# A two-layer vision network on one core: relative terms packed per head parity, and GpSimd adding the value products of the dilated attention

## Chip, cores and metric

The kernel runs on one core of a Trainium2 chip. The metric is the device time of one execution in microseconds (us), as the median of several runs. Engines are named as in the profile: PE is TensorE (PEld its weight loads), DVE is VectorE, ACT is ScalarE, POOL is GpSimd and SP is SyncE.

## What is computed

Four images of 64x64 tokens with 128 channels go through two layers. Layer 0 is a block attention with halo (8 heads of 16 channels, blocks of 8x8 queries, 12x12 keys) and a gated feed-forward part over the 2,047 best tokens. Layer 1 is a dilated attention (3x3 taps at dilations 2 and 3) and a graph attention over 524,288 edges that routes tokens to four experts. The change touches the two attentions only.

```python
# layer 0: scores of one block, plus relative terms
scores = einsum('bnhwqd,bnhwkd->bnhwqk', attn_q, key)       # q, k of 16 channels, k = 12*12
pos = rel_h[..., :, None] + rel_w[..., None, :]              # both from q and a 16x23 table
attn = softmax(scores + pos, axis=-1)
out = einsum('bnhwqk,bnhwkv->bnhwqv', attn, value)
# layer 1: nine dilated taps per pixel
attn = softmax(einsum('bndhw,bndkhw->bnkhw', qh, kw) * scale, axis=2)
out = einsum('bnkhw,bndkhw->bndhw', attn, vw)
```

## The kernel before

The program has these stages, one after the other on every engine: a sort of all edges (VectorE), then for each of the four images the first attention (`l0conv_*`), its feed-forward part (`l0ffn_*`), the dilated attention (`l1conv_*`) and the graph tables (`gat_*`); then the loop over the sorted edges, in which GpSimd gathers rows from HBM, and the last mixing of experts. Engines meet at a barrier after each part of an image. Within a part the order on each engine is the order of the code, and semaphores (`wait_ge`, `then_inc`) tie the engines together.

**First attention.** The 64 blocks of an image are 64 tiles `w`, with `h,i=w//8,w%8`: `h` is the row of blocks (called a strip here; the code's letter), `i` the block in it. All eight attention heads of a block are worked at once, four PSUM banks wide. Per tile PE runs `S(w+1)` (scores: 8 products of queries and keys, and 48 products that expand the relative terms), `weighted(w-1)` and `turn(w)` (transposes). After that comes a piece that depends on `i`: `values` in even tiles, `relative(h+1,a)` in tiles 1 and 3, `project` in tile 5, `queries` in tile 7. VectorE runs, per tile, the normalization of tile w (reciprocal and product, `norm`), the maximum over keys of tile w+1 (`mx`, L224), in tiles 2 to 5 one rounding remainder (`rest`), the copy of the transposed weights (L259) and the merge of the tile before. ScalarE takes the exponentials (L303). The scores have one set of banks, so `S(w+1)` waits for the exponentials of tile w.

`relative(h,a)` makes the relative term of a whole strip: 8 fp32 products of 64 columns with the tables `EH` (a=0) or `EW` (a=1). ScalarE copies it (L293), and it is split into three bf16 parts `ZZ[..][a][0..2]`, which the 48 products of `S` read with the indicator `INDB[a][o]`, where `o` is the parity of the attention head. Before the first tile of an image stands a prologue: queries, ten key chunks and both relative terms of strip 0.

**Dilated attention.** An image has 8 units `m`. Per unit VectorE makes 9 products of queries and shifted keys (`product`, L581), the softmax, and 9 products of expanded weights (PSUM) and shifted values (`value`, L587), eight of which it adds to an accumulator `ACC` (L590). PE sums the products into logits (L668), expands the weights for each tap (L686, four banks in turn) and projects a finished pair of units (L696, L699, bank 4). The products of unit m+1 are threaded between the values of unit m; unit 7 has none.

GpSimd issues in the meantime indirect DMAs: 128 gathers of sorted blocks during image 0 (L858, paced by `s_kv` and `s_p2`), and in images 1 to 3 32 scatters each (L954). The last 32 scatters come behind image 3.

Of the kernel before, what the change touches and what calls it, by code (L numbers as in the profile page):

```python
# [15 lines left out]
def declare_dense(nc, ctx, SA, SB):  # L16
# [759 lines left out]
def declare_nodes(nc,ctx,n,SA,m):  # L776
# [54 lines left out]
def pos_dve(dve,n,PSB,m):  # L831
# [18 lines left out]
    dve.drain()  # L850
def pos_pool(pool,m,n,d):

    I=m.SI
# [1 line left out]
    for t in range(NT):
        if t<20: pool.wait_ge(n.s_kv,t+1)
        else: pool.wait_ge(n.s_p2,(t-20)*66//108+1)
        pool.indirect_dma_start(out=I[:,t*BLK:(t+1)*BLK],out_offset=None,in_=d["SK"],in_offset=IOA(ap=m.BLKI[:,t:t+1],axis=0)).then_inc(n.gb_ld,16)  # L858
# [86 lines left out]
def edges_pool(pool,n,d,tick,V):  # L945

    pool.wait_ge(n.np_rdy,1)
    for t in range(NT):
        b,i=t//TILES,t%TILES
        if b<IMGS-1:  # L950
            if i==0: pool.wait_ge(n.ad_ld,16*(b+1))
            pool.wait_ge(n.s_p2,72*(b+1)+9*(i//4)+2*(i%4)+1)
        elif i==0: pool.wait_ge(n.ad_ld2,16)
        pool.indirect_dma_start(out=d["AEXP"],out_offset=IOA(ap=n.SIX[:,t:t+1],axis=0),in_=n.ADN[:,t,:],in_offset=None,bounds_check=4096*128-1,oob_is_err=False).then_inc(n.ad_sc,16)  # L954
# [650 lines left out]
```

## Time and profile before

| | |
|---|---|
| median of 3 runs | 7053.45 us (7039.84 to 7058.35) |
| the profiled execution | 7049.08 us, of which the span from first to last instruction is 7047.3 us |
| sort | 0 to about 980 us |
| first attention, per image | 36.8 us of prologue and 239.3 us of tiles in image 0 |
| dilated attention, per image | 199.3 to 212.7 us from the first softmax to the last residual |
| edge loop | about 3756 to 6600 us |
| last stage | about 6600 to 7047 us |

The profile's times are of one execution. "Busy" is the time in which an engine worked on an instruction; a row in brackets such as `[0.46 <-PE PSB L366]` gives the idle time of the engine just before, and the instruction whose end released it.

### The profile page before, as it was taken

Reading aid. Unit: us, or ns where it says so; the run is one execution under the profiler, and the core shown is the slowest. Engines: PE = TensorE matmul, PEld = TensorE weight load, DVE = VectorE, ACT = ScalarE, POOL = GpSimd, SP = SyncE. Lnnn points to the kernel's source line nnn. Section 1 sums busy time; section 2 is a strip of 40 time slices with the busy share of each in tenths; the row PEclk is TensorE's granted clock in tenths of the full one; section 3 lists DMA queues with packets and bytes.
Section 4 is the critical chain, followed back from the end, with each engine's and each line's share of the span. In section 5 each row is a group of like instructions: output and inputs, shape, how many; then the busy total and the mean of one; then the engine's idle time right before and its main releaser. Section 6 shows DMA issues by size and latency. Waiting matters only on the chain.

```text
span 7047.3 us, 83154 instructions
## 1 busy us (share of the span) xinstructions
PE 2995.6 (43%) x31245; PEld 1791.3 (25%) x31245; DVE 3414.0 (48%) x7000; ACT 1543.3 (22%) x3959; POOL 2605.7 (37%) x2472
## 2 busy tenths in 40 slices
PE   0011149766987897788760222222222222222204
PEld 0011138424842673376220000000000000000103
DVE  9999988576857685777661111111111111111138
ACT  0000027403730463165200111111111111111100
POOL 0000000051011000100017777777777777777450
PEclk9975569866986798698755656565655555555556
DMA  2000040002000100010022222222122222222216
GB/s 82 0 0 0 0 168 4 4 18 56 4 12 1 40 3 1 13 17 3 1 33 22 34 33 33 33 33 33 28 31 33 33 29 31 33 33 33 65 46 218
DMA packets 259879, 227.73 MB, mean 32 GB/s; under 512 B 115180, under 2 KB 223128, under 8 KB 250456
## 3 DMA queue, kind: packets, MB, share of 16 engines
q0 software_dynamic: 78944, 29.28, 6.6%
q1 hardware_dynamic: 99960, 99.91, 4.6%
q10 hardware_dynamic: 80640, 93.86, 4.3%
q8 instruction: 237, 3.88, 0.2%
q14 instruction: 98, 0.80, 0.0%
HBM read 100.42 MB, written 121.39 MB: 31 GB/s over the span
## 4 chain that ended last, share of the span: by engine, by line
PE 27%; issue 20%; another core or an unknown queue 19%; DVE 19%; DVEq 7%; ACT 4%; DMA 3%; POOL 1%; ACTq 1%; SPq 0%
DVE SA_ L1325 3%; PE PSB L382 2%; PE PSB L1175 2%; DVE SA_ L1315 2%; PE PSB L686 2%; PE PSB L668 2%; PE PSB L352 2%; PE PSB L526 2%; DVEq L1406 2%; PE PSB L392 1%; PE PSB L518 1%; DVE SA_ L590 1%; DMA VPAD<-s_TNT 1%; PE PSB L366 1%
## 5 line engine op out<-in xcount | busy, mean ns | idle before, releaser
L962 POOL DMA_INDIRECT SA_<-s_T,GIX x2048 | 2166.4, 1058 | 675.7 <-issue 675.7
L1175 PE MATMUL PSB<-VPAD,EH 128*128 128x512 f32 x512 | 302.0, 754 | 1994.1 <-DMA VPAD<-s_TNT 1643.1
L907 DVE TENSOR_TENSOR XPAD<-SA_ 128x256 f32<-128x256 f32 x32 | 13.6, 425 | 1789.9 <-DMA SA_<-s_T,GIX 1789.9
L954 POOL DMA_INDIRECT s_AEXP<-fill,SIX x128 | 149.6, 1169 | 1557.3 <-DVE SA_ L587 1472.2
L858 POOL DMA_INDIRECT SA_<-s_SK,BLKI x128 | 131.5, 1028 | 1484.3 <-PE PSB L710 1389.0
L1175 PEld LDWEIGHTS PSB<-VPAD,EH 128*128 128x128 f32 x512 | 121.6, 246 | 2195.3 <-DMA VPAD<-s_TNT 1681.4
L1179 PE MATMUL PSB<-SA_,EW 128*128 128x512 f32 x512 | 345.6, 824 | 342.1 <-ACT SA_ L1160 181.0
L1429 PE MATMUL PSB<-ident,SA_ 128*128 128x128 f32 x448 | 83.1, 368 | 837.1 <-DVE SA_ L1396 575.1
L303 ACT ACTIVATE PRX<-PSB,MX 128x144 f32<-128x144 f32 x1024 | 375.2, 380 | 210.3 <-DVE MX L224 210.1
L1164 ACT ACTIVATE VPAD<-PSB,PRX 128x512 f32<-128x512 f32 x128 | 87.9, 687 | 1308.8 <-remote 969.0
L1160 ACT ACTIVATE SA_<-PSB,PRX 128x512 f32<-128x512 f32 x256 | 175.9, 687 | 770.6 <-issue 327.0
L916 DVE TENSOR_TENSOR SB_<-SA_,SB_ 128x1024 f32<-128x1024 f32 x32 | 39.2, 1225 | 562.5 <-ACT SB_ L933 313.8
L1429 PEld LDWEIGHTS PSB<-ident,SA_ 128*128 128x128 f32 x448 | 77.4, 198 | 842.5 <-DVE SA_ L1396 579.0
L382 PE MATMUL PSB<-ident,PRX 128*72 128x128 f32 x2048 | 277.4, 279 | 1.0 <-DVE PRX L230 0.5
L1325 DVE TENSOR_TENSOR SA_<-SA_ 128x2048 f32<-128x2048 f32 (+1 forms) x124 | 254.3, 2051 | 8.6 <-issue 0.4
L1179 PEld LDWEIGHTS PSB<-SA_,EW 128*128 128x128 f32 x512 | 121.1, 250 | 539.7 <-issue 322.5
L1326 DVE TENSOR_TENSOR SA_<-SA_ 128x2048 f32<-128x2048 f32 (+1 forms) x124 | 253.4, 2044 | 0.0
L587 DVE TENSOR_TENSOR SA_<-PSB,VPAD 128x512 f32<-128x512 f32 x288 | 194.5, 685 | 119.0 <-PE PSB L686 119.0
L1347 ACT ACTIVATE SA_<-PSB 128x256 f32<-128x256 f32 x112 | 42.9, 383 | 875.6 <-PE PSB L1429 873.6
L259 DVE COPY VPAD<-PSB 72x512 f32<-72x512 f32 x256 | 175.6, 686 | 106.6 <-PE PSB L382 105.2
L382 PEld LDWEIGHTS PSB<-ident,PRX 128*72 128x72 f32 x2048 | 208.2, 116 | 53.2 <-issue 30.3
L224 DVE TENSOR_REDUCE MX<-PSB 128x4 f32<-128x576 f32 x256 | 192.9, 754 | 36.4 <-PE PSB L366 35.7
(365 smaller groups left out, 7339.3 us busy)
## 6 DMA issues: line engine op xcount, KB each, us to landing
SA_<-s_T,GIX POOLq DMA_INDIRECT x2048
s_Y<-VPAD ACTq DMA_DIRECT2D x32, 1024.0 KB
s_R<-zero SPq DMA_DIRECT2D x96, 256.0 KB, 2.9
s_R<-XPAD ACTq DMA_DIRECT2D x32, 768.0 KB
SB_<-s_Y SPq DMA_DIRECT2D x16, 1024.0 KB, 5.5
SA_<-s_Y SPq DMA_DIRECT2D x16, 1024.0 KB, 6.2
s_AEXP<-zero SPq DMA_DIRECT2D x32, 256.0 KB, 3.0
SA_<-in_x SPq DMA_DIRECT2D x16, 512.0 KB
```

Source lines behind the costliest of these rows:

```text
L224: dve.tensor_reduce(n.MX[:,w%2,:],PSB[:,0:2048].rearrange("p (j x) -> p j x",j=4)[:,:,0:144],AX.X,ALU.max,negate=True).then_inc(n.s_mx,1)
L259: dve.tensor_copy(n.PTS[:,4:8,:],PSB[0:72,5*512:6*512].rearrange("p (a q) -> p a q",a=4)).then_inc(n.s_ptd,1)
L303: last=act.activation(n.PR_[:,w%2,j,:],PSB[:,j*512:j*512+144],ACT.Exp,bias=n.MX[:,w%2,j:j+1],accum_out=n.SM[:,w%2,j:j+1])
L382: last=pe.transpose(PSB[0:72,o:o+P],n.PR_[:,w%2,j,72*g:72*g+72],ident)
L587: dve.tensor_tensor(rows(to),rows(PSB[:,bank*512:(bank+1)*512]),tap(n.VD,m,TAPS[j]),ALU.mult).then_inc(n.s_p2,1)
L962: pool.indirect_dma_start(out=n.G[:,s,c,:],out_offset=None,in_=d["T"],in_offset=IOA(ap=n.GIX[s][:,c:c+1],axis=0)).then_inc(n.gath[s],16)
L1160: act.activation(n.HM2[:,m,:],PSB[:,(m%4)*512:(m%4+1)*512],ACT.Gelu,bias=n.B1M[:,m:m+1]).then_inc(n.moe_ge,1)
L1175: pe.matmul(PSB[:,(m%4)*512:(m%4+1)*512],n.WM1[:,m//2,(m%2)*P:(m%2+1)*P],n.TNC[:,s,:],start=True,stop=True).then_inc(n.moe_h,1)
L1179: for f in range(2): last=pe.matmul(PSB[:,(4+e)*512:(5+e)*512],n.WM2[:,2*e+f,:],n.HM2[:,2*e+f,:],start=(f==0),stop=(f==1))
L1325: dve.tensor_tensor(x,a,b,ALU.min)
L1326: return dve.tensor_tensor(y,a,b,ALU.max)
L1429: last=pe.transpose(PSB[:,q*P:(q+1)*P],src[:,q*P:(q+1)*P],ident)
```

## The change

In the first attention each relative term is now made per head parity and not per table. ScalarE writes, behind the plain copy of the queries, two more copies that are masked to the even and odd heads (`QM`). `relative(h,o)` multiplies the masked queries of parity `o` with both tables, 16 products into one accumulation, with the tables' columns moved so that both lie side by side in a head pair's 32 rows. Then one indicator serves all, and `S` needs 24 products per tile where it had 48. The copy L293 becomes plain, since PE writes in the order of windows.

In the dilated attention VectorE writes the value products into a ring of four buffers `PR2` and no longer adds. GpSimd adds them (`l1conv_pool`), and issues its indirect DMAs between the adds: one gather per add in image 0 (48 gathers now come in the feed-forward part before, 20 in the key stage, 60 between adds), one scatter per two adds in images 1 to 3. `value` waits for the add four products back, and `project` for all adds of its pair of units.

```diff
+    n.PR2=[pr[:,6,:],pr[:,7,:],n.REST[:,:],SA[:,19968:20480]]
...
-        act.activation(n.QW[:,h%2,:].rearrange(WINDOWS,w=8,y=8),top.rearrange(ROWMAJOR,y=8,w=8),ACT.Copy).then_inc(n.s_qc,1)
+        act.activation(n.QW[:,h%2,:].rearrange(WINDOWS,w=8,y=8),top.rearrange(ROWMAJOR,y=8,w=8),ACT.Copy)
+        if h: act.wait_ge(n.s_p,b*16+2*h)
+        for o in range(2): last=act.activation(n.QM[o].rearrange(WINDOWS,w=8,y=8),top.rearrange(ROWMAJOR,y=8,w=8),ACT.Copy,scale=n.PAR[:,o:o+1])
+        last.then_inc(n.s_qc,1)
...
-        q=n.QW[:,h%2,:].rearrange(("c (w y x) -> c y w x","c (w y x) -> c x w y")[a],w=8,y=8)
-        for y in range(8):
-            last=pe.matmul(top[:,64*y:64*(y+1)],(n.EH,n.EW)[a][:,y,:],q[:,y,:,:],start=True,stop=True)
+        for t,form in ((n.EH,"c (w y x) -> c y w x"),(n.EW,"c (w y x) -> c x w y")):
+            q,out=(v.rearrange(form,w=8,y=8) for v in (n.QM[a],top))
+            for i in range(8):
+                last=pe.matmul(out[:,i,:,:],t[:,i,:],q[:,i,:,:],start=(i==0 and t is n.EH),stop=(i==7 and t is n.EW),skip_group_check=True)
...
-            for a in range(2):
-                for r,o,out in tiles: last=pe.matmul(out,n.ZZ[h%2][a][k][r,64*i:64*i+64],n.INDB[r,a,o,:],start=False,stop=(k==2 and a==1),skip_group_check=True)
+            for r,o,out in tiles: last=pe.matmul(out,n.ZZ[h%2][o][k][r,64*i:64*i+64],n.INDB[r,:],start=False,stop=(k==2),skip_group_check=True)
...
-        acc=n.ACC[:,m//2%2,m%2,:]; to=n.PR2[:,j%2,:] if j else acc
+        to=n.PR2[(j-1)%4] if j else n.ACC[:,m//2%2,m%2,:]
+        if j and 8*m+j>4: dve.wait_ge(n.s_ad,b*64+(8*m+j-4))
...
-        if j:
-            dve.drain()
-            last=dve.tensor_tensor(acc,acc,to,ALU.add)
-            if j==8: last.then_inc(n.s_acc,1)
...
-        if h==0: pe.wait_ge(n.s_acc,b*8+(2*u+2)); pe.wait_ge(n.s_cqc,b*8+min(2*u+5,8))
+        if h==0: pe.wait_ge(n.s_ad,b*64+8*(2*u+2)); pe.wait_ge(n.s_cqc,b*8+min(2*u+5,8))
...
+def l1conv_pool(pool,m,n,d,b):
+
+    if b: pool.wait_ge(n.ad_ld,16*b)
+    for u in range(UNITS):
+        acc=n.ACC[:,u//2%2,u%2,:]
+        for j in range(1,9):
+            k=8*u+(j-1)
+            pool.wait_ge(n.s_p2,b*72+(9*u+j+1))
+            pool.tensor_tensor(acc,acc,n.PR2[(j-1)%4],ALU.add).then_inc(n.s_ad,1)
+            if b==0 and HELD+PROJ+k<NT: block_pool(pool,m,n,d,HELD+PROJ+k)
+            if b and j%2==0: start_pool(pool,n,d,(b-1)*TILES+k//2)
+            pool.drain()
```

PE's queue in tile 1 of strip 0 in the first attention, from the scores of tile 2 to the start of those of tile 3, before. `PRX` are the weights, `VS` the values, `ident` marks transposes.

```order
L363 MATMUL PSB<-SB_,QW 64x144 x4
L363 MATMUL PSB<-SA_,QW 64x144 x4
L366 MATMUL PSB<-INDB,SA_ 64x144 x48
L392 MATMUL PSB<-VPAD,VS 32x128 x8
L382 MATMUL PSB<-ident,PRX 72x128 x8
L352 MATMUL PSB<-QW,EH 128x64 x8
L363 MATMUL PSB<-SB_,QW 64x144 x4
```

The same place in the changed kernel, where `VPAD` in the rows of L356 is the region that holds the first masked copy.

```order
L367 MATMUL PSB<-SB_,QW 64x144 x4
L367 MATMUL PSB<-SA_,QW 64x144 x4
L369 MATMUL PSB<-INDB,SA_ 64x144 x24
L395 MATMUL PSB<-VPAD,VS 32x128 x8
L385 MATMUL PSB<-ident,PRX 72x128 x8
L356 MATMUL PSB<-VPAD,EH 128x8x8 x8
L356 MATMUL PSB<-VPAD,EW 128x64 x8
L367 MATMUL PSB<-SB_,QW 64x144 x4
```

The score piece has 24 products less, and the relative piece between the transposes and the next score piece has 16 products where it had 8.

VectorE's queue in the dilated attention, from the third value product of a unit to the next softmax, before.

```order
L587 TENSOR_TENSOR SA_<-PSB,VPAD 128x512
L590 TENSOR_TENSOR SA_<-SA_ 128x512
L587 TENSOR_TENSOR SA_<-PSB,VPAD 128x512
L590 TENSOR_TENSOR SA_<-SA_ 128x512
L581 TENSOR_TENSOR SA_<-QW,SB_ 128x512
L587 TENSOR_TENSOR SA_<-PSB,VPAD 128x512
L590 TENSOR_TENSOR SA_<-SA_ 128x512
L587 TENSOR_TENSOR SA_<-PSB,VPAD 128x512
L590 TENSOR_TENSOR SA_<-SA_ 128x512
```

The same place after, to the softmax itself (`REST` is one of the four ring buffers).

```order
L591 TENSOR_TENSOR SA_<-PSB,VPAD 128x512
L591 TENSOR_TENSOR REST<-PSB,VPAD 128x512
L584 TENSOR_TENSOR SA_<-QW,SB_ 128x512
L591 TENSOR_TENSOR SA_<-PSB,VPAD 128x512 x3
L591 TENSOR_TENSOR REST<-PSB,VPAD 128x512
L591 TENSOR_TENSOR SA_<-PSB,VPAD 128x512
L602 TENSOR_REDUCE LMX<-PSB 128x32
```

The adds have left VectorE's queue. They stand in GpSimd's, here at its start in image 0.

```order
L854 DMA SA_<-s_SK,BLKI 128x64 x68
L880 ISA
L880 TENSOR_TENSOR SA_<-SA_ 128x512
L854 DMA SA_<-s_SK,BLKI 128x64
L880 TENSOR_TENSOR SA_<-SA_ 128x512
L854 DMA SA_<-s_SK,BLKI 128x64
L880 TENSOR_TENSOR SA_<-SA_,REST 128x512
```

68 gathers now stand ahead of the first add, and each further gather stands behind an add.

## Rows read from the trace of the kernel before

**Rows 1.** Windows: us, busy PE, PEld, DVE, ACT, POOL, granted clock, DMA.
```profile
1018.80:1258.10 239.30, 225.70 (x6056) 189.99 (x6060) 193.70 (x427) 177.81 (x653) 0.00 (x0) 0.99 0.17 60
2114.90:2327.50 212.60, 154.84 (x498) 55.16 (x498) 155.62 (x275) 18.04 (x31) 34.86 (x32) 0.62 0.01 1
3756.00:6600.00 2844.00, 626.14 (x992) 235.98 (x992) 335.21 (x1121) 351.95 (x462) 2166.39 (x2049) 0.58 0.21 32
```

**Rows 2.** Groups: busy, mean ns, idle before and its releaser.
```profile
L224 DVE TENSOR_REDUCE MX<-PSB 128x4 f32<-128x576 f32 x256 | 192.9, 754 | 36.4 <-PE PSB L366 35.7
L590 DVE TENSOR_TENSOR SA_<-SA_ 128x512 f32<-128x512 f32 x256 | 177.2, 692 | 24.3 <-issue 0.9
```

**Rows 3.** Timeline, strip 3, tiles 4 and 5 of image 0: start, us, engine, instruction.
```profile
1124.78 0.17 DVE L228 RECIPROCAL RSM<-SM 128x4 f32<-128x4 f32 x1
1125.70 0.75 DVE L224 TENSOR_REDUCE MX<-PSB 128x4 f32<-128x576 f32 x1
1126.82 2.06 PE L352 MATMUL PSB<-QW,EW 128*128 128x64 f32 x16
1128.35 0.18 DVE L228 RECIPROCAL RSM<-SM 128x4 f32<-128x4 f32 x1
1128.81 0.35 PE L363 MATMUL PSB<-SB_,QW 32*64 32x144 f32 x4
1129.11 0.68 PE L366 MATMUL PSB<-INDB,SA_ 32*64 32x144 bf16 x48
1129.82 0.76 DVE L224 TENSOR_REDUCE MX<-PSB 128x4 f32<-128x576 f32 x1 [0.46 <-PE PSB L366]
```

**Rows 4.** L366: who waited for it (us, times).
```profile
  DVE MX L224: 35.7, 64
```

**Rows 5.** L382: what ended PE's idle time before it (us, times).
```profile
  issue: 30.3, 153
  DVE PRX L230: 22.5, 106
```

**Rows 6.** Timeline of image 1's prologue.
```profile
1708.80 0.60 ACT L281 ACTIVATE QW<-PSB 128x512 f32<-128x512 f32 x1 [3.86 <-DMA s_ADT<-VPAD]
1711.97 0.61 ACT L293 ACTIVATE REST<-PSB 128x512 f32<-128x512 f32 x1
1712.94 2.06 PE L352 MATMUL PSB<-QW,EW 128*128 128x64 f32 x16
1714.83 3.95 PE L346 MATMUL PSB<-XPAD,WK 128*128 128x476 f32 x10
1715.84 2.25 ACT L285 ACTIVATE SB_<-PSB,PAR 128x476 f32<-128x476 f32 x3 [0.94 <-PE PSB L346]
```

**Rows 7.** Timeline of units 2 and 3, image 1's dilated attention.
```profile
2184.74 0.69 DVE L587 TENSOR_TENSOR SA_<-PSB,VPAD 128x512 f32<-128x512 f32 x1 [0.36 <-PE PSB L686]
...
2189.25 0.45 DVE L602 TENSOR_REDUCE LMX<-PSB 128x32 f32<-128x288 f32 x1
...
2199.34 1.29 DVE L587 TENSOR_TENSOR SA_<-PSB,VPAD 128x512 f32<-128x512 f32 x2 [2.61 <-PE PSB L686]
...
2207.32 0.69 DVE L587 TENSOR_TENSOR SA_<-PSB,VPAD 128x512 f32<-128x512 f32 x1 [1.33 <-PE PSB L686]
...
2214.25 0.45 DVE L602 TENSOR_REDUCE LMX<-PSB 128x32 f32<-128x288 f32 x1
```

**Rows 8.** Timeline of unit 7, image 1.
```profile
2303.50 1.29 DVE L587 TENSOR_TENSOR SA_<-PSB,VPAD 128x512 f32<-128x512 f32 x2 [3.92 <-PE PSB L686]
...
2315.37 2.04 PE L696 MATMUL PSB<-BPR,ones 1*128 1x512 f32 x2 [4.30 <-issue]
```

**Rows 9.** GpSimd's gathers: VectorE idle (first row), and beside its products.
```profile
1399.22 0.94 POOL L858 DMA_INDIRECT SA_<-s_SK,BLKI  x1 [0.30 <-issue]
...
1433.76 1.29 DVE L581 TENSOR_TENSOR SA_<-QW,SB_ 128x512 f32<-128x512 f32 x2
1433.98 1.28 POOL L858 DMA_INDIRECT SA_<-s_SK,BLKI  x1 [0.30 <-issue]
```

More of the change, by code:

```diff
@@ L70, in declare_dense @@
     n.s_gt, n.s_tb, n.x3_st, n.tn_st, n.t_st, n.sorted_ = [sem(s) for s in ("s_gt", "s_tb", "x3_st", "tn_st", "t_st", "sorted_",)]
-    n.s_acc, n.s_ltc, n.s_lt, n.s_res = [sem(s) for s in ("s_acc", "s_ltc", "s_lt", "s_res",)]
+    n.s_ad, n.s_ltc, n.s_lt, n.s_res = [sem(s) for s in ("s_ad", "s_ltc", "s_lt", "s_res",)]
     n.s_ka, n.s_kd, n.s_p, n.s_pe, n.s_c0, n.s_r, n.s_c1, n.s_z = [sem(s) for s in ("s_ka", "s_kd", "s_p", "s_pe", "s_c0", "s_r", "s_c1", "s_z",)]
-    n.INDB=sb("INDB",[P,2,2,144],bf16)
+    n.INDB=sb("INDB",[P,144],bf16); n.G4=sb("G4",[P,128,4]); n.QM=[V[:,4352:4864],n.G4[:,:,:].rearrange("p t e -> p (t e)")]
     n.bar=dict(pe=n.bar_pe,act=n.bar_act,dve=n.bar_dve)
@@ L100, in sync_weights @@
     for h in range(8):
-        for t,nm in ((n.EH,"pos_emb_h"),(n.EW,"pos_emb_w")):
+        for t,nm,o in ((n.EH,"pos_emb_h",h//2*32),(n.EW,"pos_emb_w",h//2*32+16)):
             for q in range(8):
-                ld(t[16*h:16*h+16,q,16*h:16*h+12],d[nm][:,11-q:23-q])
+                ld(t[16*h:16*h+16,q,o:o+12],d[nm][:,11-q:23-q])
     n.NW=loads
@@ L112, in dve_prep @@
     dve.tensor_scalar(n.PAR4[:,:],n.PAR[:,:],0.25,None,ALU.mult)
-    for a,ind in enumerate((n.INDH,n.INDW)):
-        for o in range(2): dve.tensor_scalar(n.INDB[:,a,o,:],ind[:,:],n.PAR[:,o:o+1],None,ALU.mult)
+    dve.tensor_scalar(n.INDB[:,:],n.INDH[:,:],n.PAR[:,0:1],None,ALU.mult); dve.drain()
+    dve.scalar_tensor_tensor(out=n.INDB[:,:],in0=n.INDW[:,:],scalar=n.PAR[:,1:2],in1=n.INDB[:,:],op0=ALU.mult,op1=ALU.add)
     dve.tensor_copy(n.DIGI[:,:],iota[:,0:16]); dve.drain()
@@ L199, in kbank @@
     return PSB[:,KB[c%6]*512:KB[c%6]*512+hi-lo]
-ROWMAJOR="p (y w x) -> p w y x"; COLMAJOR="p (x w y) -> p w y x"; WINDOWS="p (w y x) -> p w y x"
+ROWMAJOR="p (y w x) -> p w y x"; WINDOWS="p (w y x) -> p w y x"
 def l0conv_first_dve(dve,n,b):
@@ L292, in relative @@
         if h or a: act.wait_ge(n.s_z,b*16+(2*h+a))
-        act.activation(n.REST[:,:].rearrange(WINDOWS,w=8,y=8),top.rearrange((ROWMAJOR,COLMAJOR)[a],w=8,y=8),ACT.Copy).then_inc(n.s_pe,1)
+        act.activation(n.REST[:,:],top,ACT.Copy).then_inc(n.s_pe,1)
         act.drain()
@@ L850, in pos_dve, with block_pool, keys_pool @@
     dve.drain()
+HELD=48; PROJ=20
+def block_pool(pool,m,n,d,t):
+    pool.indirect_dma_start(out=m.SI[:,t*BLK:(t+1)*BLK],out_offset=None,in_=d["SK"],in_offset=IOA(ap=m.BLKI[:,t:t+1],axis=0)).then_inc(n.gb_ld,16)
 def pos_pool(pool,m,n,d):
-    I=m.SI
     pool.wait_ge(m.blk_rdy,1); pool.wait_ge(m.sk_st,16)
[L855 to L858, printed above, removed]
+    for t in range(HELD+PROJ):
+        if t<HELD: pool.wait_ge(n.s_h,t*2//3+1)
+        else: pool.wait_ge(n.s_kv,t-HELD+1)
+        block_pool(pool,m,n,d,t)
+def keys_pool(pool,m,n,d):
     pool.wait_ge(n.end_rdy,1)
@@ L862, in pos_pool, with start_pool @@
         if t>=4: pool.wait_ge(n.s_h,32+t-3)
-        pool.indirect_dma_start(out=I[:,t*128:(t+1)*128],out_offset=None,in_=rows,in_offset=IOA(ap=m.QI[:,t:t+1],axis=0)).then_inc(n.a2_ld,16)
+        pool.indirect_dma_start(out=m.SI[:,t*128:(t+1)*128],out_offset=None,in_=rows,in_offset=IOA(ap=m.QI[:,t:t+1],axis=0)).then_inc(n.a2_ld,16)
+def start_pool(pool,n,d,t):
+    pool.indirect_dma_start(out=d["AEXP"],out_offset=IOA(ap=n.SIX[:,t:t+1],axis=0),in_=n.ADN[:,t,:],in_offset=None,bounds_check=4096*128-1,oob_is_err=False).then_inc(n.ad_sc,16)
+def l1conv_pool(pool,m,n,d,b):
[9 more added lines that the diff above has]
+            pool.drain()
 def edges_prep_dve(dve,n,SA,V,ones,K,row):
@@ L945, in edges_pool @@
 def edges_pool(pool,n,d,tick,V):
[L947 to L954, printed above, removed]
+    pool.wait_ge(n.ad_ld2,16)
+    for t in range((IMGS-1)*TILES,NT): start_pool(pool,n,d,t)
     pool.wait_ge(n.d0_rdy,1)
@@ L1505, in _ @@
             pos_pool(pool,m,n,d)
+            l1conv_pool(pool,m,n,d,0)
+            keys_pool(pool,m,n,d)
+            pool.wait_ge(m.fill_done,FILLS); pool.wait_ge(n.np_rdy,1)
+            for b in range(1,IMGS): l1conv_pool(pool,m,n,d,b)
             V=blocks(pool,m)
-            pool.wait_ge(m.fill_done,FILLS)
             edges_pool(pool,n,d,m.tick,V)
```

4 lines of the change are left out of this document (2 added, 2 removed).

## The prediction

> **What bounds the kernel now.** I read the windows first, to see which stages the change can reach [rows 1]. The edge loop takes 2,844 us, its gathers and their order stay as they are, and so do the sort and the last stage: nothing there. What moves is the first attention (239.3 us of tiles in image 0, after a prologue) and the dilated attention (212.6 us in image 1), in each of four images. In the first, PE is busy 225.7 of 239.3 us at a granted clock of 0.99; in the second, VectorE is busy 155.6 of 212.6 us, and PE 154.8 us at a mean clock of 0.62, that is, in part at 1.2 GHz. So the two halves of the change meet two different limits. In the first attention the change must take work off PE, or off the loop that runs through PE, VectorE and ScalarE. In the second it takes work off VectorE, and the reader has to ask where VectorE then waits for PE or GpSimd.
>
> **First attention: the scores.** The 48 indicator products take 0.68 us [rows 3], so 24 less are worth 0.34 us a tile, and 256 tiles would give 87 us if each were bound by them. The groups say how seldom that is so: the maximum L224 waits for them 35.7 us in all, in 64 of 256 tiles [rows 2, 4]. In the other tiles the maximum follows the normalization of the tile before, which takes 0.92 us from the reciprocal to the maximum (1124.78 to 1125.70 [rows 3]) and starts when the exponentials are done, just as the scores do; the scores need 1.0 us (1128.81 to 1129.82). With them at 0.67, the normalization is what ends last. The second gain would be that the transposes come 0.34 us earlier; but in 106 tiles they already waited for the normalization, and in the 153 others (an idle of 0.20 us each) they stand close behind it [rows 5]. So outside the tiles named next I take about 0.1 us a strip, nearly nothing.
>
> **First attention: the relative terms.** This is the term that speaks against the change. `relative` goes from 8 products to 16. The trace shows 16 records for 8 fp32 products, and the next tile's scores start 1.99 us after the first (1126.82 to 1128.81 [rows 3]), with PE not idle before them. Each record has its own load of a 128x128 table, and their number doubles, so I take another 1.95 us (the EH form is some 0.1 us shorter). In this place PE is what ends last: the reciprocal that follows the exponentials stood at 1128.35, before the scores, and the maximum then waited 0.46 us for PE [rows 3]. These are the 56 tiles (2 in each of strips 0 to 6, four images) that make up most of the 64 waits [rows 4]. What the doubled piece adds lies on the path: +1.95 for the relative piece, -0.34 for the shorter scores behind it, +1.6 us. Behind this stall, what is late next is the copy of the transposed weights, the merge and the normalization: a chain that keeps its length, so nothing is made up. 56 x 1.6 = +90 us.
>
> **Prologue.** Here both relative pieces stand in a chain with the key chunks, and ScalarE has two more copies at about 0.55 us spacing ahead of the first. The queries are now ready at 1709.4; with the masked copies at 1710.6. The first piece then takes to 1714.6, where ScalarE now copies at 1711.97; the second starts after that copy, at 1715.7 in place of 1712.94, and ends at 1719.8, so the keys start 4.9 us later than 1714.83, for which ScalarE already waits 0.94 us [rows 6]. The masked copies of strip 1's queries, ahead of the first exponentials, add 1.1 us. Sum +6 us an image, +24 us. In tile 0 of a strip the masked copies hold up an exponential by some 0.2 us at most and are in the 90.
>
> Sum for the first attention: 90 + 24 - 2 = **+112 us**. Lower end: every tile but the 56 gains its full 0.34 us (200 x 0.34 = 68 us), which leaves +47. Upper end: no gain from the shorter scores at all (56 x 1.95 = 109), the prologue, and 7 us of ScalarE: +140.
>
> **Dilated attention: what VectorE loses.** The 256 adds are 177.2 us [rows 2]. Most of this isn't on the path. In unit 3 of image 1 the first value product waits 2.61 us for PE, and the fifth at 2207.32 again 1.33 us; without adds it comes to that point earlier and waits longer, since PE runs without a gap at the low clock before it. What is left of the gain is the end: from 2207.32 to the next softmax at 2214.25 are 6.93 us for five values and their adds, and five values alone take 5 x 0.69 = 3.4, a gain of 3.5 us. In a unit that closes a pair (units 2, 4 and 6) the projection holds the last three values: 2184.74 to 2189.25 is 4.51 us, and 3 x 0.69 = 2.1 leaves a gain of 2.4 us [rows 7]. The seven units with a successor: 4 x 3.5 + 3 x 2.4 = 21 us an image, 85 us in all, if GpSimd costs nothing.
>
> **What GpSimd costs.** The trace has no GpSimd add. Lower bound: VectorE's 0.69 us [rows 2]. Upper bound: I take 1.5 us, a fifth over the spacing of GpSimd's gathers, 1.25 (0.94 and 0.30 of issue [rows 9]). I choose 1.2, by the nearest row of that engine. A unit then needs 8 x (1.2 + 1.25) = 19.6 us in image 0 and 8 x 1.2 + 4 x 1.3 = 14.8 us in the others. Unit 7 has no products to fill the time, and `project` waits for its last add: from the second value at about 2304.2 GpSimd needs 14.8 us, to 2319, and the projection started at 2315.37 [rows 8]. So the end of each image is 4 to 5 us later, +18 in all.
>
> Then contention. A gather on GpSimd takes 0.94 us with VectorE idle and 1.28 beside VectorE's products of two SBUF inputs [rows 9]. The Trainium skill (SBUF — State Buffer, Who interferes with whom) says that a VectorE instruction with two SBUF inputs and a GpSimd instruction that reads SBUF exclude each other for the whole instruction; the row shows a stretch, not a whole block, and has no add. Mechanism and price here: after the last value of a unit up to four adds are outstanding, while VectorE runs the softmax with two products and one multiply of two SBUF inputs on its path. If each waits for half an add, 3 x 0.6 = 1.8 us a unit; if none, 0. I take 1.3 us, 28 units, +36 us.
>
> Sum for the dilated attention: -85 + 18 + 36 = -31; the gathers that now stand between adds in image 0 bring its unit near 22 us of the 23 to 26 it has, where GpSimd itself begins to bind, and I take 6 us off the gain: **-25 us**. Ends: adds at 0.69 us and no contention, with unit 7 some 3 us shorter, -97; every product that meets an add waits for a whole one (3 x 1.2 a unit, 101 us in place of 36), +40.
>
> The Trainium skill (GPSIMD Engine Reference, Elementwise — side-by-side cycle accounting) gives 4,497 ns for an add of 2,048 fp32 columns; a quarter, 1.12 us, is an estimate from that page. By it a unit's adds would take 0.6 us less, and the sum would be about 2 us lower.
>
> **Sum.** 112 - 25 = +87 us on the profiled execution's own 7049 us: 7136. The median of the runs is 4 us above that execution, so 7140.
>
> **Rivals.**
>
> *Contention makes the dilated attention slower too* (chance 0.13). For it: the softmax path has three exposed instructions, and image 0 has a gather per add. Against: products 2 to 5 have 2.61 us of cover, 6 to 8 more. It gives +112 + 10 to 40: 7170 to 7200.
>
> *The first attention takes only half of my cost* (0.19). For it: PE's transposes came earlier in 153 tiles, and the loads of the tables might overlap better when 16 follow each other. Against: the 16 records now follow each other at 0.12 us with nothing between. It gives +50 to 70, less 25 to 50: 7053 to 7098.
>
> *Faster* (0.07). PE's clock is what decides. It stands at 0.62 in the dilated attention; a VectorE that leaves shorter gaps may keep PE at 2.4 GHz for most of a unit. Then the waits of 2.61 and 1.33 us shrink, and a unit goes toward VectorE's own work: 18 products x 0.69 and some 4.4 us of softmax and residual, 16.8 us in place of 25. It decides where the dilated attention gains more than the first loses, 112 / 28 = 4 us a unit net of the ends; at 6 us a unit it is 168 - 112 = 56 us faster, 6997. Against: PE's long idle during the softmax, after which it stands at half clock, stays.
>
> *The relative terms aren't dearer*, as the name of the change may suggest (24 products in place of 48) and PE gets lighter: refuted by the counts, 64 pieces x 1.95 = +125 us of PE against 87.
>
> **How the numbers follow.** The forecast's own case (first attention +90 to +140, dilated -60 to 0) has 0.61: 7083 to 7190. A measurement of this kernel tells 0.3%, 21 us, from no change. Faster than 7032: the third rival and a sliver of the second, 0.08. Within 21 us: the low part of the second rival, 0.13. Slower: 0.79. The range leaves out about 0.1 on either side: 7055 to 7192.
>
> **What the changed profile would show.** Relative pieces of 32 records and about 3.95 us, with the next scores right behind; waits of the maximum for PE of about 2 us in 56 tiles, over 100 us in all where it has 35.7; 63 tile periods of an image in about 261 us in place of 239.3; a prologue 6 us longer. In the dilated attention: units of 22 to 24 us, GpSimd adds near 1.2 us, VectorE products longer or started late where an add runs, and 4 to 5 us more before the last projection. Wrong would be I if a relative piece took 2.5 us, if an add took over 2 us (then GpSimd binds every unit), or if PE's clock rose above 0.8 there.

## The result, and the profile after

The changed kernel takes 7209.32 us (median of 4 runs, 7205.4 to 7213.07), the kernel before, run beside it, 7048.49 (7039.84 to 7058.35): a ratio of 1.0228, 95% interval 1.021 to 1.0245. It is slower by 161 us. The profiled execution spans 7203.6 us against 7047.3: +156.

The stages of both traces, read off the timelines (first product of queries, first and last maximum L224 of an image, first softmax maximum L602 of unit 0 and of unit 7, last residual), images 0 to 3 in order. The prologue counts here from the first product of queries; "36.8 us" for image 0 in the table of the kernel before also holds what stands ahead of that product.

| stage | before, us | after, us | change |
|---|---|---|---|
| first attention, prologue | 17.2, 18.4, 17.2, 17.2 | 20.6, 24.7, 28.1, 21.0 | +24 |
| first attention, tiles 0 to 63 | 239.3, 237.1, 238.5, 237.0 | 257.3, 257.7, 257.9, 257.1 | +78 |
| feed-forward part | 76.1 each | 87.9, then 76.1 to 76.3 | +12 |
| dilated attention, units 0 to 6 | 176.9, 180.2, 166.8, 178.3 | 223.8, 158.2, 158.4, 161.1 | +47 in image 0, -48 in the others |
| dilated attention, unit 7 and ends | 35.8, 32.4, 32.4, 32.4 | 51.8, 42.4, 42.2, 41.8 | +45 |

The rest (key stages, edge loop, last stage) is the same within 3 us in all. After, the windows of the first attention of image 0 and of the dilated attention of images 1 and 0 answer to [rows 1]:

```profile
1023.40:1280.60 257.20, 239.44 (x4764) 202.72 (x4768) 191.39 (x427) 185.51 (x667) 0.00 (x0) 0.99 0.14 49
2243.70:2444.30 200.60, 137.23 (x498) 50.96 (x498) 124.67 (x211) 17.99 (x31) 120.28 (x96) 0.67 0.01 1
1458.20:1733.80 275.60, 148.98 (x498) 56.17 (x498) 121.82 (x211) 18.07 (x31) 143.27 (x124) 0.61 0.03 7
```

VectorE's busy time in the dilated attention fell from 155.6 to 124.7 us, and GpSimd's rose from 34.9 to 120.3. Image 1 gained 12 us by it; image 0, with the same VectorE time, lost 63.

In the first attention the stall came in the tiles that were forecast. Strip 3, tile 5, in the timeline of image 0, beside [rows 3]:

```profile
1132.44 1.90 PE L356 MATMUL PSB<-VPAD,EH 128*128 128x64 f32 x16
1134.17 2.09 PE L356 MATMUL PSB<-VPAD,EW 128*128 128x64 f32 x16
1136.19 0.35 PE L367 MATMUL PSB<-SB_,QW 32*64 32x144 f32 x4
1136.49 0.48 PE L369 MATMUL PSB<-INDB,SA_ 32*64 32x144 bf16 x24
1137.00 0.76 DVE L224 TENSOR_REDUCE MX<-PSB 128x4 f32<-128x576 f32 x1 [2.20 <-PE PSB L369]
```

32 records and 3.75 us from the first to the next scores, where there were 16 and 1.99; the maximum waits 2.20 us for PE instead of 0.46. Over the kernel, the groups beside [rows 2] (busy, mean ns, idle before and its releaser):

```profile
L224 DVE TENSOR_REDUCE MX<-PSB 128x4 f32<-128x576 f32 x256 | 192.7, 753 | 124.5 <-PE PSB L369 124.5
L880 POOL TENSOR_TENSOR SA_<-SA_ 128x512 f32<-128x512 f32 x192 | 256.4, 1335 | 1269.2 <-DVE SA_ L591 1123.5 <-issue 127.0 <-DVE REST L591 18.7
L584 DVE TENSOR_TENSOR SA_<-QW,SB_ 128x512 f32<-128x512 f32 x288 | 229.4, 844 | 20.4 <-PE PSB L668 20.1
L591 DVE TENSOR_TENSOR SA_<-PSB,VPAD 128x512 f32<-128x512 f32 x224 | 149.1, 686 | 201.1 <-PE PSB L686 114.6 <-POOL SA_ L880 86.5
```

The wait of L224 for PE went from 35.7 us in 64 tiles to 124.5 in 66. The last row is new: VectorE's value products now wait 86.5 us for a buffer that a GpSimd add must free (and 47.1 us more for the buffer `REST`), and the products of QW and keys take 844 ns where they took 685.

How far the adds lie apart is seen in image 0's timeline (GpSimd and the value products):

```profile
1575.09 1.26 POOL L880 TENSOR_TENSOR SA_<-SA_ 128x512 f32<-128x512 f32 x1 [1.64 <-issue]
1576.45 0.69 DVE L591 TENSOR_TENSOR SA_<-PSB,VPAD 128x512 f32<-128x512 f32 x1 [3.30 <-POOL SA_ L880]
1576.49 0.95 POOL L854 DMA_INDIRECT SA_<-s_SK,BLKI  x1
1578.98 1.26 POOL L880 TENSOR_TENSOR SA_<-SA_,REST 128x512 f32<-128x512 f32 x1 [1.54 <-issue]
```

An add takes 1.26 us and a gather 0.95, as expected. But the next add starts 1.5 to 1.6 us after the gather has ended: 3.9 us from add to add where the prediction had 2.45. Over the whole kernel the pause between an indirect DMA and the next add, where GpSimd waited for nothing else, has a median of 1.47 us and is mostly between 1.3 and 1.9. In image 1's unit 7, with a scatter behind every second add:

```profile
2411.69 1.29 DVE L591 TENSOR_TENSOR SA_<-PSB,VPAD 128x512 f32<-128x512 f32 x2 [3.91 <-PE PSB L686]
...
2424.13 1.25 POOL L880 TENSOR_TENSOR SA_<-SA_ 128x512 f32<-128x512 f32 x1 [1.30 <-issue]
2425.55 1.26 POOL L880 TENSOR_TENSOR SA_<-SA_ 128x512 f32<-128x512 f32 x1 [0.17 <-issue]
2426.97 1.00 POOL L871 DMA_INDIRECT s_AEXP<-fill,SIX  x1 [0.15 <-issue]
2429.29 1.25 POOL L880 TENSOR_TENSOR SA_<-SA_,REST 128x512 f32<-128x512 f32 x1 [1.32 <-issue]
...
2432.07 2.04 PE L696 MATMUL PSB<-BPR,ones 1*128 1x512 f32 x2 [14.11 <-issue]
```

Behind an add and its drain alone the next add starts after 0.17 us; behind an add, a scatter and the drain after 1.32. A pair of adds takes 5.16 us (2424.13 to 2429.29). From unit 7's first values to the projection are 20.4 us (2411.69 to 2432.07), where [rows 8] had 11.9.

### The profile page after: what moved, and what is told of

The parts are those of the page before. It is cut to its first block, busy times and chain, and to the rows that moved or that the text cites. A ratio compares the mean times of both kernels' runs of the same rounds, so it can differ in the third digit from the quotient of the medians.

```text
span 7203.6 us, 73219 instructions
## 1 busy us (share of the span) xinstructions
PE 3050.7 (42%) x26125; PEld 1849.9 (26%) x26125; DVE 3288.4 (46%) x6742; ACT 1578.1 (22%) x4023; POOL 2939.2 (41%) x2728
## 4 chain that ended last, share of the span: by engine, by line
PE 24%; another core or an unknown queue 22%; issue 17%; DVE 17%; DVEq 7%; ACT 5%; DMA 4%; POOL 2%; POOLq 2%; ACTq 1%; SPq 0%
DVE SA_ L1335 3%; PE PSB L356 3%; PE PSB L1185 3%; DVE SA_ L1325 2%; PE PSB L385 2%; PE PSB L686 2%; DMA VPAD<-s_TNT 2%; POOLq L883 2%; PE PSB L668 2%; ACT PRX L306 2%; DVEq L1416 1%; PE PSB L529 1%; PE PSB L521 1%; POOL SA_ L880 1%
## 5 line engine op out<-in xcount | busy, mean ns | idle before, releaser
L880 POOL TENSOR_TENSOR SA_<-SA_ 128x512 f32<-128x512 f32 x192 | 256.4, 1335 | 1269.2 <-DVE SA_ L591 1123.5
L1174 ACT ACTIVATE VPAD<-PSB,PRX 128x512 f32<-128x512 f32 x128 | 87.9, 687 | 1308.2 <-remote 981.0
L224 DVE TENSOR_REDUCE MX<-PSB 128x4 f32<-128x576 f32 x256 | 192.7, 753 | 124.5 <-PE PSB L369 124.5
L591 DVE TENSOR_TENSOR SA_<-PSB,VPAD 128x512 f32<-128x512 f32 x224 | 149.1, 686 | 201.1 <-PE PSB L686 114.6
L584 DVE TENSOR_TENSOR SA_<-QW,SB_ 128x512 f32<-128x512 f32 x288 | 229.4, 844 | 20.4 <-PE PSB L668 20.1
```

The costliest lines, as they stand in the source:

```text
L224: dve.tensor_reduce(n.MX[:,w%2,:],PSB[:,0:2048].rearrange("p (j x) -> p j x",j=4)[:,:,0:144],AX.X,ALU.max,negate=True).then_inc(n.s_mx,1)
L584: dve.tensor_tensor(rows(n.PRD[:,(9*m+j)%6,:]),rows(n.QW[:,m%2,:]),tap(n.KD,m,TAPS[j]),ALU.mult).then_inc(n.s_pr,1)
L880: pool.tensor_tensor(acc,acc,n.PR2[(j-1)%4],ALU.add).then_inc(n.s_ad,1)
```

## The experiments

The runs fall in two groups. In group A, that of the result and of e9 to e12, the kernel before takes 7045 to 7048 us; in group B, e1 to e8, it takes 6722 to 6729. The edge loop, which no run changes, takes 2841 us in the traces of A and 2609 in those of B. What sets the groups apart is not known: the record numbers the chips of e1 to e12 as 6 and 14 in B and as 6 and 9 in A, so the number of a chip alone does not tell them apart. Each run is compared with the kernel before that was run beside it. There is no trace of the kernel before in B; stages in B are compared with e1, whose dilated attention is that of before: units 0 to 6 in 166.9, 167.8, 171.5 and 169.6 us, unit 7 and ends in 31.8 to 32.8.

**e1: the first half alone** (the kernel before with the packed terms).

> The change of the first attention alone; the dilated attention, its adds and the gathers as before. My theory (the two halves add up, and the first costs what the longer relative pieces put on the path): the tiles of each image 18 to 21 us longer, the prologues together 24 us, nothing in the feed-forward part of image 0; about 102 us over before, 7150 us. Rival (the halves interact, and most of the loss comes with the adds): under 40 us over before.

Measured (B): 6821.18 us, ratio 1.015 [1.0127, 1.0173], +99 us. Tiles 257.4 to 258.1 us, 20 more than before's as expected, prologues 20.6, 26.7, 26.3 and 20.6, +24 in sum.

**e2: the second half alone** (the adds on GpSimd, first attention as before).

> The change of the dilated attention alone (GpSimd adds, the gathers moved); the first attention as before. My theory: image 0 loses 63 us in the dilated attention (a unit of 32 us) and 12 us in the feed-forward part, where 48 gathers now run; images 1 to 3 gain 48 us in units 0 to 6 and lose 29 us behind unit 7: about 55 us over before, 7105 us. Rival (the halves interact): more than 20 us away from that, or no stall in the feed-forward part.

Measured (B): 6786.85 us, ratio 1.0088 [1.0068, 1.0109], +64 us. Image 0: units 223.3 us, end 52.0; the others 155.7 to 161.4 and 41.8 to 42.5. The expected stall in image 0's feed-forward part did not come (76.1 us). Each half alone makes the kernel slower. 99 and 64 add up to 163, and the whole change is 161 in A. That the halves don't disturb each other is made likely by this and not shown, since the halves ran in B only, and the second one is made up differently there: against e1, image 0's units cost 56 us, the ends 49, the other units gain 34, and the feed-forward part costs nothing.

**e3: e2 with the drain ahead of the DMA.**

```diff
             pool.tensor_tensor(acc,acc,n.PR2[(j-1)%4],ALU.add).then_inc(n.s_ad,1)
+            pool.drain()
             if b==0 and HELD+PROJ+k<NT: block_pool(pool,m,n,d,HELD+PROJ+k)
             if b and j%2==0: start_pool(pool,n,d,(b-1)*TILES+k//2)
-            pool.drain()
```

> As the run with the adds alone, but GpSimd's drain stands directly behind its add and the indirect DMA behind the drain, so that no drain follows a DMA before the next add. My theory (the drain behind a DMA costs the 1.3 to 1.5 us that GpSimd stands idle before each next add, which an add alone shows as 0.17 us): an add and a gather take about 2.7 us in place of 4.0, image 0's units fall from 32 us to 22 to 24, and the ends of images 1 to 3 get 4 to 5 us shorter: about 80 us below the adds alone, 7025 us. Rival (an add cannot start until the DMA's descriptors are written, with or without a drain): the spacing stays 4.0 us and the time within 10 us of the adds alone.

Measured (B): 6761.83 us, ratio 1.0048 [1.0029, 1.0067], 25 us below e2; 80 were expected. Image 0 moved the way that was said, but half as far: its units take 26 to 28 us each, 188.1 instead of 223.3 in all, where 22 to 24 each were expected. The rival, that the spacing stays at 4.0 us, is out. From one add to the next:

```profile
1571.75 1.27 POOL L877 TENSOR_TENSOR SA_<-SA_ 128x512 f32<-128x512 f32 x1
1573.90 0.95 POOL L851 DMA_INDIRECT SA_<-s_SK,BLKI  x1 [0.88 <-issue]
1574.87 1.27 POOL L877 TENSOR_TENSOR SA_<-SA_ 128x512 f32<-128x512 f32 x1
```

3.1 us instead of 3.9, and 2.7 expected. The add now follows the DMA at once, but the DMA starts 0.85 to 1.1 us after the add, where it followed in 0.15; a pair with one scatter is still 4.65 us, so the ends of images 1 to 3 lose only 2 us (image 0, with a gather behind every add, 7), and the units of images 1 to 3 grew to 164.9 to 168.6. There the products of QW and keys are longer than in e2 (window 2114 to 2327, first row e2, then e3):

```profile
L581 DVE TENSOR_TENSOR SA_<-QW,SB_ 128x512 f32<-128x512 f32 x72 | 59.8, 878 | 2.7 <-PE PSB L665 2.5
```

```profile
L581 DVE TENSOR_TENSOR SA_<-QW,SB_ 128x512 f32<-128x512 f32 x72 | 69.1, 1008 | 2.5 <-PE PSB L665 2.4
```

What is saved at the drain is paid back in part in these products (e7 and e8 show what stretches them), and the sequence of add, drain and DMA is dear in either order.

**e4: e1 with 8 products per relative piece** (half of each relative term is left out).

```diff
-        for t,form in ((n.EH,"c (w y x) -> c y w x"),(n.EW,"c (w y x) -> c x w y")):
+        for t,form in (((n.EH,"c (w y x) -> c y w x"),(n.EW,"c (w y x) -> c x w y"))[a],):
```

> As the run with the first attention's change alone, but each relative piece keeps 8 of its 16 products: parity 0 gets only the row table, parity 1 only the column table, the other half of the relative term is left out. The scores keep 24 products. It separates the shorter scores from the longer relative pieces. My theory (the longer pieces carry the whole loss, and shorter scores give almost nothing): tiles within 3 us an image of before, prologues 2 to 3 us longer for the masked copies, 7045 to 7065 us. Rival (each shorter score piece gives its 0.34 us): about 17 us less an image, 6985 us.

Measured (B): 6704.63 us, ratio 0.9971 [0.9957, 0.9985], -18 us. Tiles 231.4 to 232.6, 6 us an image below before, so neither theory is right: mine had said within 3 us an image, the rival 17 less. Of the 24.5 us that the four images' tiles lose, 17.5 lie in the 56 tiles behind a relative piece (0.31 us each), and 7 in the 196 other tiles (under 0.04 us each): the shorter scores give what the rival says only where the maximum waits for PE. e1 has the second 8 products of each piece too and takes 117 us more, 104 of them in the tiles.

**e5: e2 with no DMA between adds.** All 128 gathers of image 0 come ahead of its dilated attention, and the scatters in the feed-forward parts.

```diff
-HELD=48; PROJ=20
+HELD=108; PROJ=20
...
-        if t<HELD: pool.wait_ge(n.s_h,t*2//3+1)
+        if t<HELD: pool.wait_ge(n.s_h,t*8//27+1)
...
+    for t in range(TILES if b else 0): pool.wait_ge(n.s_h,b*32+t+1); start_pool(pool,n,d,(b-1)*TILES+t)
...
-            if b==0 and HELD+PROJ+k<NT: block_pool(pool,m,n,d,HELD+PROJ+k)
-            if b and j%2==0: start_pool(pool,n,d,(b-1)*TILES+k//2)
```

> Second half of the change alone (the dilated attention's sums on GpSimd, first attention as before), with all 128 gathers of image 0 issued ahead of its dilated attention (108 in the feed-forward part, 20 in the key stage) and the 32 scatters per image issued in the feed-forward part, so that no DMA stands between two sums. Theory 1, what costs time is the drain behind an indirect DMA on GpSimd (1.3 to 1.5 us against 0.17 us) and the DMA itself (1.0 us): the spacing of sums falls to 1.42 us, units 0 to 6 of image 0 take 150 to 160 us instead of 223, those of images 1 to 3 stay at or under 158, unit 7 and the ends take 32 to 35 us instead of 42 (52 in image 0); against the kernel before 45 to 70 us less. Theory 2, GpSimd's sums slow VectorE down and the DMAs are innocent: image 0 stays at 200 us or more, the ends at 40 us or more, and the time stays 40 to 65 us above before. Rival within theory 1: the 60 gathers moved into the feed-forward part lengthen that part (76 us) or the key stage (25 us).

Measured (B): 6711.38 us, ratio 0.9971 [0.9961, 0.9981]: 75 us below e2 and 17 below before, where 45 to 70 below before were expected. The ends are 34.1 to 34.6 us (42 to 52 in e2), so theory 1 holds there. Image 0's units took 195.2 us, not 155: its first unit was 58 us, since the first add stood behind gathers that ran until 1461. The units of images 1 to 3 (159.6, 154.6, 156.2) are no shorter than in e2, although the adds are 1.42 us apart: something else holds them.

**e6: e5 with unit 7's adds on VectorE.**

```diff
+        if m==UNITS-1 and j:
+            dve.drain()
+            last=dve.tensor_tensor(n.ACC[:,m//2%2,m%2,:],n.ACC[:,m//2%2,m%2,:],to,ALU.add)
+            if j==8: last.then_inc(n.s_ad,1)
...
-    for u in range(UNITS):
+    for u in range(UNITS-1):
...
```

> As e5, but the eight sums of unit 7 of every image stay on VectorE behind their products, as in the kernel before; GpSimd does those of units 0 to 6. If the ends grew only because GpSimd paced the last sums, the ends come to 32.4 us as before and the rest equals e5: the time is within 6 us of e5, lower by whatever e5's ends are above 32.4 us. Against the kernel before 55 to 75 us less. If the ends are longer than 35 us here too, something other than GpSimd's pace makes them long.

Measured (B): 6705.34 us, ratio 0.9967 [0.9953, 0.9981]. 23 us below before, not the 55 to 75 expected, since the first unit of image 0 takes 57.9 us here too. Ends 33.3 to 33.7, within 1.5 us of e1's. e5 and e6 are equal within their intervals: without DMAs in between, GpSimd ends unit 7 nearly as early as VectorE.

**e7: e5 without the adds** (left out of the computation; GpSimd only counts).

> As e5, but GpSimd only counts: the eight sums per unit are left out of the computation altogether, so neither VectorE nor GpSimd does them. It prices what GpSimd's sums cost VectorE. Theory A, contention: the products QW x KD (878 ns each with sums on GpSimd, 684 ns alone, 72 per image) fall back to 684 ns, and units 0 to 6 shorten by 10 to 20 us per image against e5, 40 to 80 us in all. Theory B, contention is hidden because TensorE sets the pace: the products fall to 684 ns but the units shorten by less than 3 us per image, under 12 us in all.

**e8: e5 with each add replaced by a fill with zeros** (adds left out; GpSimd writes and doesn't read).

> As e5, but each of GpSimd's sums is replaced by a fill with zero of the buffer that it would have read (the sums are left out of the computation): it only writes and reads nothing. If it is GpSimd's reading of SBUF beside VectorE's two SBUF operands that stretches the products, they take 684 ns as in e7; if any GpSimd work on SBUF does, they stay above 780 ns. Time between e7 and e5; I expect within 10 us of e7.

Measured (B): e7 6627.13 us (0.9841 [0.9815, 0.9866]), e8 6624.34 (0.984 [0.9818, 0.9861]), both 84 to 87 us below e5. Units of images 1 to 3: e7 139.0, 140.8, 149.3; e8 142.0, 140.7, 144.5; e5 159.6, 154.6, 156.2. The products of VectorE, groups over the kernel, in e5:

```profile
L581 DVE TENSOR_TENSOR SA_<-QW,SB_ 128x512 f32<-128x512 f32 x288 | 258.5, 946 | 8.2 <-PE PSB L665 7.8
L588 DVE TENSOR_TENSOR SA_<-PSB,VPAD 128x512 f32<-128x512 f32 x224 | 148.0, 684 | 171.1 <-PE PSB L683 124.9 <-POOL SA_ L878 46.2
```

and in e8:

```profile
L581 DVE TENSOR_TENSOR SA_<-QW,SB_ 128x512 f32<-128x512 f32 x288 | 183.0, 684 | 16.0 <-PE PSB L665 15.6
L588 DVE TENSOR_TENSOR SA_<-PSB,VPAD 128x512 f32<-128x512 f32 x224 | 148.3, 686 | 168.7 <-PE PSB L683 128.4 <-POOL SA_ L878 40.3
L878 POOL MEMSET SA_<- 128x512 f32 x192 | 100.8, 525 | 621.1 <-DVE SA_ L588 601.0 <-DVE REST L588 5.5 <-issue 5.4
```

Theory A holds: the products with both inputs in SBUF are stretched by GpSimd's adds (946 ns on average, 1789 at most, against 684) and not by its fills, which only write; value products, with one input in PSUM, stay at 684 to 686 beside either. Theory B falls, since units 0 to 6 shorten by 7 to 22 us an image. The Trainium skill (SBUF — State Buffer, Who interferes with whom) says that a VectorE instruction with two SBUF inputs contends with a GpSimd instruction that reads SBUF and not with one that only writes it, and e5, e7 and e8 agree. In units 0 to 6, e5 and e7 differ by 63 us, 2.3 us a unit, and so do e5 and e8. Some 13 us of the 63 are value products that wait longer for GpSimd to free a buffer in e5 than in e7; the rest goes with the stretch.

**e9: e6 with the gathers from the first attention on**, two per tile (`pool.wait_ge(n.s_qk,t//2+1)`).

> As e6, but the 128 gathers of image 0 are issued from the first tile of its first attention on, two per tile, so that the last is out before the dilated attention begins. In e5 and e6 the first unit of image 0 took 54 to 58 us against 20 to 22 us in the other images, because the first sum of GpSimd stood behind gathers that ran until 1461 us. If that is all, the first unit of image 0 falls to about 22 us, the span falls by 33 to 36 us against e6, and the kernel is 50 to 65 us faster than before on the same chip (ratio 0.990 to 0.993). Rival: the gathers beside the first attention delay it (their 1.25 us each are on an idle engine, but their transfers share the queues with the image loads and the fill): then its tiles take more than 240 us and part or all of the 35 us is given back.

**e10: the changed kernel again.**

> The changed kernel as it is, beside the kernel before on the chip of this call. If the two halves add up (e1 +99 us, e2 +64 us), it is 160 to 167 us above the kernel before. The stall of 12 us in image 0's feed-forward part (87.9 us instead of 76.1 us in the first profile) is either part of the change (87.9 us here too) or was chance (76.1 us).

Measured (A): e9 7010.55 us, ratio 0.995 [0.9936, 0.9963], 35 us below before where 50 to 65 were expected; e10 7207.57, ratio 1.023 [1.0214, 1.0246], +162. In e9 the first unit is 19.3 us and image 0's units take 156.3, as said; but the rival came too: its first attention took 255.3 us, and image 1's feed-forward part 102.1. e10 had the longer feed-forward part in image 0 again (87.4), so in A that is no chance.

**e11: e9 with the DMAs thinner; e12: e6 again**, beside each other.

```diff
-        pool.wait_ge(n.s_qk,t//2+1)
+        if t<64: pool.wait_ge(n.s_qk,t+1)
+        elif t<HELD: pool.wait_ge(n.s_h,(t-64)*2//3+1)
+        else: pool.wait_ge(n.s_kv,t-HELD+1)
...
-    for t in range(TILES if b else 0): pool.wait_ge(n.s_h,b*32+t+1); start_pool(pool,n,d,(b-1)*TILES+t)
+    for t in range(TILES if b else 0): pool.wait_ge(n.s_qk,b*64+2*t+1); start_pool(pool,n,d,(b-1)*TILES+t)
```

> As e9, with the indirect DMAs of GpSimd spread thinner: the gathers of image 0 are issued one per tile of its first attention (64), 44 in its feed-forward part and 20 in the key stage; the 32 scatters of the image before are issued one per two tiles of the first attention, not in the feed-forward part. e9 left 16 us in image 0's first attention (255.3 us instead of 239.3) and 26 us in image 1's feed-forward part (102.1 us instead of 76.1), with waits of VectorE for which the trace names no partner while these DMAs were issued densely. If density is the cause, both come back wholly or mostly: image 0's first attention 240 to 246 us, image 1's feed-forward part 76 to 80 us, and the kernel is 25 to 40 us below e9's distance to before, a ratio of 0.989 to 0.992. If any indirect DMA there costs its part, the delays move with them to the first attention of images 1 to 3 and the ratio stays at 0.994 to 0.997.

> The kernel of e6 again, beside e11 on the same chip, so that the two are compared by their stages: e11 should have a first unit of image 0 of about 20 us against 58 us here and otherwise the same units and ends.

Measured (A): e11 7011.01 us, ratio 0.9948 [0.9934, 0.9962], the same as e9; e12 7101.3, ratio 1.0073 [1.0057, 1.0088], though the same kernel was faster than before in B. e12's first unit is 19.3 us and not the 58 expected, because its feed-forward part took so long that the gathers of that part were out before the units began. e11's first attention came back to 240.0 us; its feed-forward part in image 0 rose to 82.8 and the key stage to 33.4 (25.0 in e9). Image 1's feed-forward part stayed at 104.6: the scatters follow the 32 key gathers in GpSimd's program, so the new waits were long over and they still came there, in a run of 36 DMAs without a pause. In images 2 and 3 e11's 32 scatters did move into the first attention, and its tiles took 237.2 and 238.0 us: spread thinly they cost nothing there (before: 238.5 and 237.0). e12 shows the cost at its clearest, in the window of image 0's feed-forward part, with 108 gathers (same columns as above; first e12 in A, then e6 in B):

```profile
1297.10:1462.50 165.40, 80.86 (x184) 36.82 (x182) 42.58 (x174) 27.78 (x41) 102.78 (x108) 0.72 0.08 22
```

```profile
1297.60:1373.70 76.10, 66.16 (x184) 31.76 (x182) 42.56 (x175) 28.76 (x41) 56.04 (x59) 0.90 0.10 25
```

VectorE does the same work in 165.4 and in 76.1 us. e12's chain of waits there is

```profile
1314.01 15.20 another core or an unknown queue
...
1331.95 23.88 another core or an unknown queue
...
1380.53 31.27 another core or an unknown queue
```

VectorE and ScalarE stand still with no partner that the trace names, while GpSimd issues a gather every 1.25 us in either group. In e12 GpSimd stands still twice as well, for 6.8 and 6.7 us, and VectorE goes on about 6 us after the last gather of the run before that (1349.8 and 1406.7, then VectorE at 1355.9 and 1412.8). In e6 113 DMAs in a row did no harm.

## Why the prediction was wrong

It said +87 us, 7140, with a range up to 7192; it is +156 on the profiled execution and 7209 in the median. The direction was right, and so was most of the first attention. What failed is the price of a GpSimd round in the dilated attention.

**First attention: right in its mechanism, with small errors in size.** "56 x 1.6 = +90 us", prologue +24, little elsewhere, +112; measured +78 and +24, and e1 gives +99 alone. The waits fell in the tiles named: from one maximum to the next, these 56 tiles take 85 us more, 1.52 each. The relative piece grew by 1.84 us on average (1.91 to 3.75; I had 1.95). The shorter scores gave 0.20, not 0.34: from the first score product to the maximum that waits for it are 1.01 us before and 0.81 after, while I had halved the busy time of the products. The transposes came 0.12 us earlier, where I had nothing. The other tiles gave 7 us instead of 2. e4 shows the same two parts, and its 0.31 us in the 56 tiles is no new gain, since my 1.6 had already taken off 0.34. The lower end that I gave for this half, +47, is +46 by its own terms; nothing hangs on it.

That the prologue came to +24 is in part luck. I had 6 us in every image; it is 3.4, 6.3, 10.9 and 3.8. In image 1 ScalarE's first copy also waits 5.56 us for the DMA `s_ADT<-VPAD`, where it waited 3.86 [rows 6], and e2, which leaves the prologue as it was, has 23.2 us there too.

**Dilated attention, image 0: the step that failed.** "A unit then needs 8 x (1.2 + 1.25) = 19.6 us in image 0", and later "where GpSimd itself begins to bind, and I take 6 us off the gain". The add was right (1.26 us) and so was the gather (0.95). What was missing is the drain at the end of each round, which I costed at nothing: behind a DMA it takes 1.5 us in the median, where it takes 0.17 behind an add alone. Eight rounds of 3.9 to 4.0 us make a unit of 32 us, and GpSimd doesn't begin to bind, it binds wholly. Units 0 to 6 of image 0 took 47 us more than before, where the sum had some 6 us less. e3 (3.1 us a round, 35 us back) and e9, e11 and e12 (no DMA between adds: 156.2 to 156.3 us for units 0 to 6) show it. My own sign of being wrong, an add of over 2 us, did not come; I had named only the add and not the round.

**The ends of images: mis-sized by the same omission.** "GpSimd needs 14.8 us", and "+18 in all" (from 2319 and 2315.37 the end would be 3.6 us later, not the 4 to 5 that I took). It needs four pairs of 5.16, 20.6 us, and in image 0, with a gather behind every add, the end grew by 16; in all the ends cost +45. e5 takes the DMAs out and the ends fall to 34.

**What VectorE loses, and contention: both too small, in opposite directions.** "85 us in all" for 28 units is 21 an image. In B, e7 against e1 gives -79.8 in images 1 to 3 alone, 26.6 us an image; where in a unit the rest is gained was not traced. Contention, "I take 1.3 us", is 2.3 a unit by e5 and e7 (the waits of value products for GpSimd are in it). It eats half of the gain: e5 against e1 is -38.5 us in images 1 to 3. In the changed kernel the two together gave -48 there in A, and e2 against e1 gave -34 in B, against about -36 by my terms. So the two errors nearly cancel, which is luck.

**+12 us in image 0's feed-forward part**, to which 48 gathers were moved: costed at nothing. It is absent in B (76.1 in e2) and there again in e10 in A. The prediction had no term for gathers beside another stage.

Sum in A: +102 first attention, -48 in images 1 to 3, +47 in image 0, +45 ends, +12 feed-forward: +158 of +156. My rival "contention makes the dilated attention slower too" had the sign and nearly the size of the second half (+10 to +40 against +44), by another mechanism: contention was real, but what turned a gain of 48 us in images 1 to 3 into a loss of 44 in all was the rounds of add, DMA and drain, in image 0's units (+47) and at the ends (+45).

**What stays open** is the cause of the waits without a partner in group A. They come in stages beside which GpSimd issues indirect DMAs closely, and how closely seems to matter: e12's feed-forward parts of images 2 and 3, with 32 scatters in groups of four to eight, take 76.1 to 76.2 us, while that of image 1, where 36 DMAs stand in a row, takes 104.6. The kernel before may have such a wait too, since its key stage of image 0, with 20 gathers, takes 37.2 us in A and that of e1 25.1 in B. Group A is also slower in the edge loop, which lives on the same kind of DMA, but slower transfers don't explain it: in image 0's feed-forward part and key stage the last packet of a gather ends 2.04 us after GpSimd starts on it in e12 and 2.02 in e6, in the median. In the loop it is GpSimd itself that issues less evenly, with 123 pauses of over 0.4 us in the kernel before and none in e1. No run tells whether the engines wait for instructions, for semaphores or for something else.

## What to carry to other kernels

Before moving work to an engine, write down everything that stands between two of its instructions, drains and DMAs too, and look for the price of that sequence and not of its parts. Where GpSimd reads SBUF, VectorE's products with two SBUF inputs took 946 ns instead of 684 here; those with one input in PSUM kept their time, and so did all of them beside GpSimd's fills. Of this change worth keeping is the second half with the DMAs out of the adds and unit 7 left where it was: e9 and e11 are 0.5% faster than before, 35 us, in the group where the whole change is 2.3% slower. The packed terms would give 18 us if the relative piece could keep its 8 products (e4, which leaves out half of each term); no run has a complete kernel of that kind.

## What the hardware did that I had not expected

- A drain on GpSimd costs 0.17 us behind an add and mostly 1.3 to 1.9 us behind an indirect DMA; a DMA behind a drain starts 0.85 to 1.1 us after the add, without it 0.15.
- A GpSimd add of 128x512 takes 1.26 us in the median and a fill of the same size 0.53; VectorE's product with two SBUF inputs goes from 684 to 946 ns on average beside the adds.
- The same program with 108 gathers in the feed-forward part is 0.3% faster than before in one group of runs and 0.7% slower in the other, with single waits up to 31 us.
